# A two-directional Mamba block with a quantised FFN: step size and dtx replicated together, B and C tiles loaded together, the weight's sum taken ahead of the first product

## The reference

```python
xz = einsum('bld,ed->ble', h, W_in);  x, z = split(xz)        # 256 inner channels each
x = silu(causal_conv(x, conv_w) + conv_b)                      # 4 taps
dt, B, C = split(einsum('bld,ed->ble', x, Wx), [64, 16, 16])
dt = softplus(einsum('blr,dr->bld', dt, Wdt) + bdt)            # step size, 256 channels
A = -exp(A_log)                                                # 256 channels x 16 states
h_t = exp(dt_t * A) * h_{t-1} + (dt_t * x_t) * B_t             # 256 x 16 states, over 1024 tokens
y_t = sum over states of h_t * C_t  +  x_t * D
out = einsum('bld,ed->ble', y * silu(z), W_out)
```

## Time and profile before

| | |
|---|---|
| median of 3 runs | 1043.89 us |
| the profiled execution's own time | 1041.62 us |
| its span, first to last instruction | 1039.8 us |
| VectorE busy | 906.6 us, 87% |
| GpSimd busy | 856.6 us, 82% |
| TensorE, ScalarE busy | 669.3 us (64%), 598.6 us (58%) |
| mean granted TensorE clock | 0.791 |
| DMA, 16 engines | 109.56 MB in 84071 packets, 105 GB/s over the span |

### The profile page before, as it was taken

The page is one execution under the profiler, slowest core; times in us unless marked ns, Lnnn a source line. Parts: engine busy times, 40 slices in busy tenths (PEclk is TensorE's granted clock), DMA queues, the critical chain, the costliest instruction groups (busy, mean ns, idle before and its releaser), DMA issues. The chain is left out here.

```text
span 1039.8 us, 9415 instructions
## 1 busy us (share of the span) xinstructions
PE 669.3 (64%) x2124; PEld 221.2 (21%) x2124; DVE 906.6 (87%) x1004; ACT 598.6 (58%) x974; POOL 856.6 (82%) x384
## 2 busy tenths in 40 slices
PE   6537637777667666677567666778576676556432
PEld 3212102222212212122112121213121221012122
DVE  2268769999999999999999999999999999999936
ACT  3436544756476665665476766665575756554414
POOL 0169579999798999999799999997998999997602
PEclk9858867788888788788789889688779788666656
DMA  2344404444343424443453424443433424441002
GB/s 57 99 129 127 143 22 118 140 110 137 95 130 94 130 83 127 133 124 114 114 142 82 137 74 134 127 129 109 120 99 97 142 75 135 124 133 49 0 1 81
DMA packets 84071, 109.56 MB, mean 105 GB/s; under 512 B 21040, under 2 KB 34352, under 8 KB 84016
## 3 DMA queue, kind: packets, MB, share of 16 engines
q1 hardware_dynamic: 84016, 108.97, 38.1%
HBM read 38.65 MB, written 3.15 MB: 40 GB/s over the span
## 5 line engine op out<-in xcount | busy, mean ns | idle before, releaser
L440 POOL TENSOR_TENSOR dbx<-dtx_rep,b_rep 128x1024 f32<-128x1024 f32 x256 | 612.6, 2417 | 63.7 <-DMA dtx_rep<-dtx 45.6
L629 ACT ACTIVATE da_ps<-dt_rep,neg_a 128x512 f32<-128x512 f32 x512 | 350.4, 688 | 339.2 <-DVE hs L892 335.1
L892 DVE TENSOR_TENSOR_SCAN hs<-da_ps,dbx 128x512 f32<-128x512 f32 x256 | 296.9, 1207 | 46.2 <-POOL dbx L440 19.8
L892 DVE TENSOR_TENSOR_SCAN hs<-da_ps,carry,dbx 128x512 f32<-128x512 f32 x256 | 312.2, 1267 | 26.8 <-issue 14.3
L1142 PE MATMUL y_ps<-ch,stack 128*32 128x512 f32 x1024 | 178.4, 775 | 209.7 <-DVE ch L782 135.5
L450 POOL TENSOR_TENSOR ch<-hs,c_rep 128x1024 f32<-128x1024 f32 x96 | 226.1, 2356 | 28.6 <-issue 13.9
L782 DVE TENSOR_TENSOR ch<-hs,c_ps 128x1024 f32<-128x1024 f32 x160 | 191.4, 1196 | 0.0
L1133 PE MATMUL c_ps<-x_dbl,select 128*128 128x512 f32 x256 | 179.5, 789 | 0.0
L1085 PE MATMUL pre<-h_t,w_conv 128*128 128x512 f32 x256 | 120.5, 614 | 7.6 <-ACT xs L530 6.4
L1142 PEld LDWEIGHTS y_ps<-ch,stack 128*32 128x32 f32 x1024 | 24.8, 120 | 324.2 <-issue 220.2
L1133 PEld LDWEIGHTS c_ps<-x_dbl,select 128*128 128x128 f32 x256 | 47.0, 229 | 146.2 <-issue 133.8
(11 more groups left out here) (125 smaller groups left out, 507.7 us busy)
## 6 DMA issues: line engine op xcount, KB each, us to landing
dt_rep<-dt SPq DMA_DIRECT2D x512, 64.0 KB, 2.1
dtx_rep<-dtx SPq DMA_DIRECT2D x512, 64.0 KB, 2.6
b_rep<-bc_rows SPq DMA_DIRECT2D x64, 256.0 KB
c_rep<-bc_rows SPq DMA_DIRECT2D x64, 256.0 KB
h_in<-in_L_attn_hidden_states SPq DMA_DIRECT2D x4, 512.0 KB, 5.6
h_res<-in_L_attn_hidden_states SPq DMA_DIRECT2D x4, 512.0 KB, 6.7
out<-hs SPq DMA_DIRECT2D x4, 512.0 KB, 2.9
bc_rows<-x_dbl SPq DMA_DIRECT2D x16, 64.0 KB, 4.7
```

The costliest lines, as they stand in the source:

```text
L440: nc.gpsimd.tensor_tensor(dbx[:, n % RING], dtx_rep[:, r], b_rep[:, k, :].unsqueeze(1).to_broadcast([P, 2, CHUNK]), ALU.mult).then_inc(dbx ...
L629: nc.scalar.activation(da_ps[:, half % DA_BANKS, :], dt_rep[:, r, e, :], ACT.Exp, scale=neg_a[:, half_of(unit), 2 * (unit % 2) + e, g, k:k ...
L892: nc.vector.tensor_tensor_scan(in_scan_order(hs[:, n % RING, e, :], s), in_scan_order(da_ps[:, (2 * n + e) % DA_BANKS, :], s), in_scan_ord ...
```

## The change

The step size and dtx now lie side by side in one tile `step`, in rows of 2 x 512 numbers (4 KB), and one set of copies replicates both; likewise B and C lie side by side in DRAM and are loaded with one DMA of 512 KB a tile. A load waits for what both of the old loads waited for. The order on SyncE is new. The FFN weight is loaded right behind the forward convolution's weights, its rows are summed after the second copy of the convolution weights, and GpSimd adds over the partitions ahead of its first product. The diff, cut where it only renames:

```diff
-        dt = sb("dt", [P, DT, CHUNK])
-        dtx = sb("dtx", [P, DT, CHUNK])
+        step = sb("step", [P, DT, 2, CHUNK])
+        dt, dtx = step[:, :, 0, :], step[:, :, 1, :]
...
+        step_rep = sb("step_rep", [P, 2 * DT, 2, 2, CHUNK])
+        dt_rep, dtx_rep = step_rep[:, :, :, 0, :], step_rep[:, :, :, 1, :]
+        bc_rep = sb("bc_rep", [P, STATES // QUAD, 2, CHUNK])
+        b_rep, c_rep = bc_rep[:, :, 0, :], bc_rep[:, :, 1, :]
...
-        bc_rows = nc.dram_tensor("bc_rows", (NG, 2 * STATES, CHUNK), f32).ap()
+        bc_rows = nc.dram_tensor("bc_rows", (NG, STATES, 2, CHUNK), f32).ap()
...
             load_conv(FWD, conv_in)
+            sp.dma_start(w_raw[:], w_ffn).then_inc(w_raw_in, 16)
...
-            sp.dma_start(w_raw[:], w_ffn).then_inc(cols_in, 16)
...
+                sp.dma_start(bc_rows[s].rearrange("n c t -> c n t"), x_dbl[0:2 * STATES, s % 2, :]).then_inc(rows_stored, 16)
...
+            def load_step(b, s, r):
                 group = NG * b + s
                 sp.wait_ge(dtx_ready, group + 1)
                 if group:
+                    sp.wait_ge(da_ready, 2 * (UNITS * (group - 1) + last_of_slot(r) + 1))
                     sp.wait_ge(dbx_ready, UNITS * (group - 1) + last_of_slot(r) + 1)
                 for e in range(2):
                     k = BLOCK * (2 * (r % 2) + e)
                     for i in range(QUAD):
+                        sp.dma_start(step_rep[BLOCK * i:BLOCK * (i + 1), r, e], step[k:k + BLOCK, r // 2]).then_inc(step_in[r], 16)
...
+            def load_bc(b, s, k):
                 group = NG * b + s
                 sp.wait_ge(rows_stored, 16 * (group + 1))
                 if group:
                     sp.wait_ge(dbx_ready, UNITS * (group - 1) + last_of_quad(k) + 1)
                     sp.wait_ge(ch_pool, pool_c(*before(b, s), last_of_quad(k) + 1))
+                rows = bc_rows[s, QUAD * k:QUAD * (k + 1)].rearrange("n c t -> n (c t)")
+                sp.dma_start(bc_rep[:, k].rearrange("p c t -> p (c t)"),
+                             rows.unsqueeze(1).to_broadcast([QUAD, BLOCK, 2 * CHUNK])).then_inc(bc_in[k], 16)
...
                     if group:
-                        load_dt(b, s, 2)
-                        load_dt(b, s, 3)
-                        load_c(b, s, 3)
+                        load_step(b, s, 2)
+                        load_step(b, s, 3)
+                        load_bc(b, s, 3)
...
                     store_rows(*nxt)
+                    load_step(*nxt, 0)
+                    load_step(*nxt, 1)
+                    for k in range(STATES // QUAD - 1):
+                        load_bc(*nxt, k)
...
             store_rows(0, 0)
+            load_bc(0, 0, 0)
+            load_step(0, 0, 0)
+            load_step(0, 0, 1)
             for k in range(1, STATES // QUAD):
+                load_bc(0, 0, k)
             for r in (2, 3):
+                load_step(0, 0, r)
...
-                        if first and s == 1 and n == 0:
-                            pool.wait_ge(w_sum, 1)
-                            nc.gpsimd.partition_all_reduce(tiny[:, 1:2], tiny[:, 0:1], P, REDUCE.add).then_inc(w_sum_all, 1)
...
+            pool.wait_ge(w_sum, 1)
+            nc.gpsimd.partition_all_reduce(tiny[:, 1:2], tiny[:, 0:1], P, REDUCE.add).then_inc(w_sum_all, 1)
             for n in range(B_AHEAD):
                 times_b(0, 0, n)
...
             nc.vector.tensor_copy(w_conv[:, FWD, 2:4, :].rearrange("p k e -> p (k e)"), y_ps[:, 1, :]).then_inc(w_conv_sb, 1)
+            dve.wait_ge(w_raw_in, 16)
+            nc.vector.tensor_reduce(tiny[:, 0:1], w_raw[:], X, ALU.add, apply_absolute_value=True).then_inc(w_sum, 1)
```

More of the change, by code:

```diff
@@ L215, in build @@
              "rstd_last_ready final_ready stored").split()]
[L218 to L221, removed]
+        bc_in = [sem(f"bc_in{k}") for k in range(STATES // QUAD)]
+        step_in = [sem(f"step_in{r}") for r in range(2 * DT)]
         block = ctx.enter_context(nc.Block())
@@ L433, in times_b @@
                 if k == 0:
-                    pool.wait_ge(dtx_in[r], 2 * QUAD * 16 * (group + 1))
+                    pool.wait_ge(step_in[r], 2 * QUAD * 16 * (group + 1))
                 if half_of(n) == 0:
-                    pool.wait_ge(b_in[k], 16 * (group + 1))
+                    pool.wait_ge(bc_in[k], 16 * (group + 1))
                 if not (group == 0 and n < RING):
@@ L445, in times_c @@
                 group, k = NG * b + s, quad_of(n)
-                pool.wait_ge(c_in[k], 16 * (group + 1))
+                pool.wait_ge(bc_in[k], 16 * (group + 1))
                 pool.wait_ge(scanned, 2 * (UNITS * group + n + 1))
@@ L554, in prepare @@
                         for k in range(2 * DT):
[L555 removed]
+                            act.wait_ge(step_in[k], 2 * QUAD * 16 * q)
                         act.wait_ge(dtx_ready, q)
                     nc.scalar.preload_act_table_set(SOFTPLUS)
[L558 removed]
+                    nc.scalar.activation(dt, u[:], ACT.Softplus).then_inc(dt_ready, 1)
                     nc.scalar.preload_act_table_set(EXP)
@@ L627, in batch @@
                             if k == 0 and e == 0:
-                                act.wait_ge(dt_in[r], 2 * QUAD * 16 * (group + 1))
+                                act.wait_ge(step_in[r], 2 * QUAD * 16 * (group + 1))
                             nc.scalar.activation(da_ps[:, half % DA_BANKS, :], dt_rep[:, r, e, :], ACT.Exp,
@@ L685, in _ @@
             act.wait_ge(a_ready, 1)
-            act.wait_ge(cols_in, 16 * 5)
+            act.wait_ge(cols_in, 16 * 4)
             batches(act, batch)
@@ L771, in prepare @@
                         for k in range(2 * DT):
-                            dve.wait_ge(dtx_in[k], 2 * QUAD * 16 * q)
-                    nc.vector.tensor_tensor(dtx[:], dt[:], xs[:, par], ALU.mult).then_inc(dtx_ready, 1)
+                            dve.wait_ge(step_in[k], 2 * QUAD * 16 * q)
+                    nc.vector.tensor_tensor(dtx, dt, xs[:, par], ALU.mult).then_inc(dtx_ready, 1)
             def times_c(b, s, n):
@@ L925, in _ @@
             constants()
-            dve.wait_ge(cols_in, 16 * 5)
+            dve.wait_ge(cols_in, 16 * 4)
             scale_w_in(REV)
-            nc.vector.tensor_reduce(tiny[:, 0:1], w_raw[:], X, ALU.add, apply_absolute_value=True).then_inc(w_sum, 1)
             batches(dve, batch)
```

57 lines of the change are left out of this document (2 added, 55 removed).

## The result

The changed kernel takes 1139.99 us in the median of 4 runs (1136.51 to 1144.34), against 1043.99 for the kernel before beside it: a ratio of 1.0916, 95% interval 1.0867 to 1.0965. It is slower by 96 us; the forecast was 1023, 21 us faster. The profiled execution took 1139.9 us with a span of 1138.1.

A forecast was written before the change was run, and what follows sets the result against it. VectorE, 87% busy, was taken to set the pace after the start. 1041.6 - 14.3 (all-reduce) - 14.1 (start) + 8 (steady part) = 1021.2, with 2.3 for the median some 1023 us; 1017 to 1030 at 50%, 1013 to 1038 at eight in ten.

The forecast's parts named there:

- All-reduce ahead: Sum over partitions moved before GpSimd's first product, into idle time; removes VectorE's 14.27 us wait in group 1: -14.3 us.
- Start: First group: fewer copy issues and joined tiles bring unit 5's product 14.0 us ahead, VectorE with it: -14.1 us.
- The 1.7 us behind the last issue: Start: assumed delay from slot 0's last copy issue to GpSimd's first product; 1.54 us in the old profile.
- Steady (a): Group boundary: step tiles of slots 0 and 1 wait for dtx instead of the softplus; up to 1.3 us late.
- Steady (b): Group boundary: tile 2 lands 7.5 us behind unit 13's C product, wanted after 7.0.
- Steady (c): Group boundary: tile 3, behind 16 step issues, lands 18.6 us after the C product, wanted at 15.3; about +8 us in all.
- x: GpSimd's wait for tile 3 at unit 6, in each of 15 groups: 3.3 to 3.6 us.
- The queue packets' price: Time per 2 KB step packet on the four engines, 0.084 us; at 0.17 for 4 KB, no addition to tile 3's lateness.
- Leads of 3.7 us: GpSimd's least lead over VectorE, at unit 15 of a third-kind group; was to hide part of GpSimd's lateness.
- Operands strided: GpSimd's product operands become strided between a unit's two halves; claimed cost 0.
- The slower one: Rival, 7%: 4 KB packets queue at 0.26 us on the four engines, delaying tile 3 by 5.7 us: 1056 us.
- The fit of the Trainium skill: Alternative: 2.0 us plus bytes over 436 GB/s; 512 KB land in 3.2 us, no wait for tile 3, whole 1015.5.

The follow-up runs named there:

- e1: The kernel before with only the weight's DMA, its sum and the all-reduce moved early as in the change: 1031.04 us, ratio 0.9879.
- e7: e1 plus step size and dtx in one tile with one set of copies, B and C still apart: 1024.81 us, ratio 0.9815.
- e12: e4 with tile 3 issued ahead of the step copies of slots 2 and 3 and rows stored by two DMAs: 1007.04 us, ratio 0.9645.
- e15: The changed kernel with the rows stored by two DMAs, B's and C's, instead of one: 1147.81 us, ratio 1.0999.
- e13: e3 with the step copies of slots 2 and 3 issued only when tile 2 has landed: 1073.41 us, ratio 1.0283.
- e4: The changed kernel with each B and C tile loaded by four DMAs, one row to 32 partitions each: 1012.30 us, ratio 0.9682.
- e14: e13 plus second buffers for tiles 1 and 2 of B and C in even groups: 1034.88 us, ratio 0.9898.
- e3: The changed kernel with tile 3 of B and C issued ahead of the step copies of slots 2 and 3: 1113.18 us, ratio 1.0669.
- e5: The changed kernel with each 128 KB step copy cut into two issues of 64 KB: 1357.63 us, ratio 1.3011.

## Why the prediction was wrong, step by step

- **All-reduce ahead, -14.3: right.** -12.9 in e1; the operation stands in idle time at 9.8 us, and VectorE's gap is gone.
- **Start, -14.1: about 5 came.** The first product was to start at 36.4 to 38.8: 42.76. The 1.7 us behind the last issue holds in e7 and e12 (1.8) and fails beside a 512 KB tile (7.9, with the tile issued 3.0 us ahead of the copies; e15's stands 6.1 ahead, and there it is 1.8). The transposed store costs 1.8 us, which I had given nothing: from store to tile 1.65 us before and in e7, 3.42 here, 2.05 with two DMAs. Tile 1 was to land at 47.2 and came at 53.1, with copies on either side of it on SyncE.
- **Steady (a), the step tiles' later start: right.** GpSimd never waits for them after the start.
- **Steady (b), "tile 2 lands 7.5 us behind the C product", is the step that failed.** It took 12 to 15. I had seen that C's wait now holds B, and I had the 16 copies on SyncE right behind the tile; I asked only whether the copies' backlog delays tile 3 and never put it to tile 2, which is in flight when they start. e13 brings 7.5 to 9.7 back by holding the copies.
- **Steady (c), tile 3 at 18.6 us, x = 3.3 to 3.6: 24 to 27.** The queue packets' price (0.084 us) came from a stretch with 64 KB copies behind finished or small broadcasts. At 128 KB an issue the engines get twice the bytes a us from SyncE, and beside the tile all of them are full for the whole 11 us (share 1.03, 156 GB/s), 4 KB at 0.43 us where I had 0.17 (and 0.29 for the copies alone in e4). Why packets are that slow beside a tile on four engines is open. GpSimd stands 178.4 - 8.2 (the start) = 170 us at 15 boundaries, 11.3 each in two places instead of 3.6 in one: 4.5 at unit 6, where the forecast had its wait, and 6.9 at unit 4, where it had 0.5. Leads of 3.7 us hide little of that. The kernel ends 114 us later for it (1140 against e1's 1031 less the start's 5), and in VectorE's account 15 of these are its longer products for dtx, for which the forecast has no term.
- **Operands strided, 0: right.** GpSimd is busy 855.0 us against 856.6; its products with B take 2.38 us for 2.42, those with C 2.43 for 2.36.
- **The rivals.** The slower one named the place and the mechanism, contention on the four engines, and priced it at 1056 with 7%. It missed by its size for the same reason: one wait a group, from tile 3 alone. The fit of the Trainium skill, "DMA: Bandwidth & Descriptors", section "Anatomy of one DMA", gave 1015.5, an estimate: its 3.2 us for 512 KB do not hold for a tile on four engines (7.5 to 9.7 in e13). For the copies and tiles of 128 KB on all of them in e4 (median 2.3 and 2.7 us from issue to landing) it gives 2.3, and the trace agrees within 0.4.

The 96 us, then: 13 and 5 gained, 114 lost. Taken away in turn, the loss falls by 27 (order, and with it 18 us of VectorE's work), 40 (copies beside tile 2), 38 (C's buffer wait), to 1034.9; the other way round, buffers first, 48, 50 and 7. They are not additive. All three cost this much only because a tile is a single DMA on four engines: e4 leaves all three in place and is at 1012.3. (e4 makes a tile wider and splits it at once; that the width does it is read from the shares, no run splits a tile and leaves it on four engines.) The last 10 us between e14 and e7 are not taken apart; ScalarE's wait, 23.4 us against 6.2 in e7, may be in them.

## What to carry to other kernels

Before two loads are joined, write down for each buffer the earliest moment at which it may be overwritten and the moment at which it is wanted: the joined load has the latest of the first and the earliest of the second. A share of 0.26 while a long DMA runs alone was the sign that it used a quarter of the engines here; splitting it by its outer dimension was worth more than everything that the joining could give or take. And whatever is issued right behind a transfer can be part of that transfer's price.

## What the runs showed of the hardware that I had not expected

- A tile's landing depends on what is issued behind it: 512 KB on four engines land 7.5 to 9.7 us behind the C product with only the next tile behind them (e13), 12 to 16 us with sixteen 128 KB copies as well (the changed kernel and e3).
- The copies suffer too. Alone in e4 they move 226 GB/s through full engines; beside a tile on four engines, in the changed kernel, tile and copies together move 156 through engines as full.
- A store of 64 KB whose outermost dimension is 2 holds up what waits for it 1.8 us longer than one of 32 rows (3.42 us against 1.65), and two stores of 16 rows 0.4 longer (2.05, e15).
- Four times as many issues for the tiles (16 a group in place of 4, some 0.5 us each) cost nothing in e4, since SyncE had room; twice as many for the copies (64 in place of 32) cost over 200 us in e5, since everything else stood behind them.
